# Where the second layer's last 4000 weight columns are loaded, rounded and split

## The reference, cut to what matters

```python
xn = _layernorm(x)
x = x + _L0_attn_ref(xn, ...) + _L0_ffn_ref(xn, ...)   # decay attention; 16 experts, top 2
xn = _layernorm(x)
x = x + _L1_attn_ref(xn, Wqkv, bqkv, Wo, bo) + _L1_ffn_ref(xn, A, B, Wr)
# _L1_attn_ref:
qkv = einsum('bsc,cf->bsf', x, Wqkv) + bqkv
out = softmax(q k^T / sqrt(128)) v;  return out @ Wo + bo
# _L1_ffn_ref:
top_vals, top_idx = top_k(xf @ Wr.T, 16);  gates = softmax(top_vals)
h = einsum('nd,krd->nkr', xf, A)                         # 64 adapters of rank 16
out = einsum('nkr,kdr->nd', h * G[:, :, None], B) * 2.0
```

## Time and profile before

| what | value |
|---|---|
| runs (us) | 2504.53, 2501.66, 2505.94; median 2504.53 |
| profiled execution | 2507.46 us, of it the span 2505.6 us |
| granted TensorE clock, mean | 0.995 |
| busy: PE, PEld, DVE, ACT, POOL | 98%, 85%, 63%, 54%, 63% |
| DMA | 183.87 MB, mean 73 GB/s |
| 2200 to 2220 us: PE busy | 2.16 us of 20 |

### The profile page before, as it was taken

The page is one execution under the profiler, slowest core; times in us unless marked ns, Lnnn a source line. Parts: engine busy times, 40 slices in busy tenths (PEclk is TensorE's granted clock), DMA queues, the critical chain, the costliest instruction groups (busy, mean ns, idle before and its releaser), DMA issues.

```text
span 2505.6 us, 42357 instructions
## 1 busy us (share of the span) xinstructions
PE 2447.8 (98%) x13850; PEld 2120.9 (85%) x13850; DVE 1574.2 (63%) x2449; ACT 1359.2 (54%) x2696; POOL 1582.6 (63%) x1523
## 2 busy tenths in 40 slices
PE   8999999999999999999999999999999999969999
PEld 6888888898989898788888888898888878857787
DVE  6565565757574657876556565757565778865553
ACT  5556555556565555555656555656555557743332
POOL 5666767676676764767776777777686578741210
PEclk9999999999999999999999999999999999989999
DMA  4210211111111113211111111111111178941110
GB/s 161 86 56 30 63 53 39 54 46 54 38 59 42 52 46 101 86 55 56 36 58 54 38 54 46 54 38 59 42 54 44 47 267 293 298 134 42 34 34 34
DMA packets 89196, 183.87 MB, mean 73 GB/s; under 512 B 12626, under 2 KB 38882, under 8 KB 89110
## 3 DMA queue, kind: packets, MB, share of 16 engines
q1 hardware_dynamic: 80566, 165.94, 20.5%
q0 software_dynamic: 8544, 16.82, 2.3%
HBM read 163.81 MB, written 26.79 MB: 76 GB/s over the span
## 4 chain that ended last, share of the span: by engine, by line
PE 86%; DVE 5%; issue 3%; SPq 3%; DMA 1%; ACT 1%; POOL 1%; DVEq 0%; POOLq 0%; ACTq 0%
PE bank L103 27%; PE bank L105 26%; PE bank L104 26%; PE bank L1118 2%; PE bank L1145 2%; SPq L2291 1%; DMA exin<-xn_rows,ecur 0%; DMA y_slots<-ey 0%; DVE acc L2880 0%; PE bank L2720 0%; DVE xl L586 0%; POOL acc L2184 0%; DVE el L2444 0%; SPq L2301 0%; PE bank L2731 0%
## 5 line engine op out<-in xcount | busy, mean ns | idle before, releaser
L2040 POOL TENSOR_TENSOR wl<-w_in,wh 128x512 fp32r<-128x512 f32 x510 | 621.9, 1246 | 304.5 <-ACT wh L1444 301.6
L103 PE MATMUL bank<-xh,wh 128*128 128x512 f32 x1400 | 556.9, 398 | 0.6 <-DVE bank L1751 0.5
L105 PE MATMUL bank<-xh,wl 128*128 128x512 f32 x1400 | 545.7, 390 | 0.0
L104 PE MATMUL bank<-xl_sums,wh 128*128 128x512 f32 x800 | 312.3, 390 | 0.0
L105 PEld LDWEIGHTS bank<-xh,wl 128*128 128x128 f32 x1400 | 262.9, 188 | 56.7
L103 PEld LDWEIGHTS bank<-xh,wh 128*128 128x128 f32 x1400 | 263.5, 188 | 52.8 <-DVE bank L1751 4.2
L2058 POOL TENSOR_TENSOR sqacc<-sqacc,sq 128x512 f32<-128x512 f32 x128 | 173.2, 1353 | 198.9 <-ACT sq L1429 194.4
L1444 ACT CAST wh<-w_in 128x512 fp32r<-128x512 f32 x502 | 262.0, 567 | 32.2 <-POOL w_in L534 32.2
L103 PE MATMUL bank<-wh,xh 128*128 128x256 f32 x912 | 259.0, 284 | 0.2
L104 PE MATMUL bank<-wl,xh 128*128 128x256 f32 x912 | 258.2, 283 | 0.0
L1788 DVE TENSOR_TENSOR acc<-bank,acc 128x512 f32<-128x512 f32 x240 | 162.2, 685 | 118.7 <-PE bank L105 116.6
(11 more groups left out here) (387 smaller groups left out, 6379.6 us busy)
## 6 DMA issues: line engine op xcount, KB each, us to landing
w_in<-in_w_pairs_dram SPq DMA_DIRECT2D x100, 512.0 KB, 3.8
o_in<-in_o_pairs_dram SPq DMA_DIRECT2D x32, 512.0 KB, 3.5
eraw<-in_ex_dram SPq DMA_DIRECT2D x31, 513.0 KB
y_slots<-ey SPq DMA_DIRECT2D x30, 512.0 KB
w_in<-in_w_pairs_dram SPq DMA_DIRECT2D x56, 256.0 KB, 3.0
dcur<-in_decay_dram SPq DMA_DIRECT2D x32, 256.0 KB
eraw<-in_ex_dram SPq DMA_DIRECT2D x31, 256.0 KB
out_dram<-acc SPq DMA_DIRECT2D x16, 256.0 KB, 2.0
```

The lines of the kernel that those rows point to most:

```text
L103: pe.matmul(out, wh, mh, start=start and i == 0, stop=False, skip_group_check=True)
L104: pe.matmul(out, wh, ml, start=False, stop=False, skip_group_check=True)
L105: ins = pe.matmul(out, wl, mh, start=False, stop=stop and i == n - 1, skip_group_check=True)
L2040: pool.tensor_tensor(wl[:, cols], w_in[:, cols], wh[:, cols].bitcast(F32), ALU.subtract).then_inc(w_lo, 1)
```

## The change

SP no longer loads the 4000 columns at tile 27. In the second layer it waits until the last gathered rows of group 0 have landed, then issues the four loads of 1000 columns, ahead of `bo` and `sel`. ACT rounds in eight pieces of 500 columns, three ahead of `score` 0, three ahead of `scores_t` and two ahead of `score` 1 of group 0; ahead of the first it waits for all four loads. POOL subtracts in eight pieces: four ahead of the first four gathers of group 1, four ahead of the other four. These last gathers now stand ahead of POOL's bias additions for group 0. PE waits piece by piece in `outputs(0, i)`.

```diff
-LATE = 4
-LATE_COLS = (L_USED - L_CUT) // LATE
+LATE_COLS = (L_USED - L_CUT) // NR
...
             is_tile, i, _, n = tile(r, b, 0)
-            if isinstance(i, int) and i == NTILES - LATE:
-
-                for k in range(LATE):
-                    c = slice(k * LATE_COLS, (k + 1) * LATE_COLS)
-                    sp.dma_start(w1_late[:, c], l1_w[:, L_CUT + c.start:L_CUT + c.stop]).then_inc(dma_l1[0], 16)
...
+    late_high = {("score", 0, 0): (0, 1, 2), ("scores_t", 0, 0): (3, 4, 5), ("score", 0, 1): (6, 7)}
...
             pe.wait_ge(q["v_hl"], NR * g + i + 1)
-            if g == i == 0:
-                pe.wait_ge(lo_late, PIECES + LATE)
+            if g == 0:
+                pe.wait_ge(lo_late, PIECES + i + 1)
...
     def scalar(a):
-
-        a.wait_ge(dma_late, 16 * (-(-PIECES // 2) + LATE))
-        for c, src in late_cols:
-            a.copy(w1h[:, c], w1_late[:, src]).then_inc(a_late, 1)
         for what, g, i in events:
+            for k in late_high.get((what, g, i), ()):
+                cols, src = late_cols[k]
+                if k == 0:
+                    a.wait_ge(dma_late, 16 * ((PIECES + 1) // 2 + NR // 2))
+                a.copy(w1h[:, cols], w1_late[:, src]).then_inc(a_late, 1)
...
     def vector(v):
-        for k, (cols, src) in enumerate(late_cols):
-            v.wait_ge(a_late, PIECES + k + 1)
-            v.tensor_tensor(w1l[:, cols], w1_late[:, src], w1h[:, cols].bitcast(F32), ALU.subtract).then_inc(lo_late, 1)
...
+        def late_low(*ks):
+            for k in ks:
+                cols, src = late_cols[k]
+                pool.wait_ge(a_late, PIECES + k + 1)
+                pool.tensor_tensor(w1l[:, cols], w1_late[:, src], w1h[:, cols].bitcast(F32),
+                                   ALU.subtract).then_inc(lo_late, 1)
...
+        late_low(0, 1, 2, 3)
+        gather(1, 0)
         pool.wait_ge(dma_sel, 80)
...
         for g in range(NG):
+            if g == 0:
+                late_low(4, 5, 6, 7)
+                gather(1, 1)
...
-            if g + 1 < NG:
+            if 0 < g < NG - 1:
                 gather(g + 1, 0)
                 gather(g + 1, 1)
...
         sp.dma_start(bq[:], b_qkv).then_inc(dma_c, 16)
 
+        sp.wait_ge(dma_y[1][TPG - 1], 16)
+        for k in range(NR // 2):
+            c = slice(2 * k * LATE_COLS, 2 * (k + 1) * LATE_COLS)
+            sp.dma_start(w1_late[:, c], l1_w[:, L_CUT + c.start:L_CUT + c.stop]).then_inc(dma_late, 16)
```

More of the change, by code:

```diff
@@ L133, in two_layers @@
         w1_late = nc.alloc_sbuf_tensor_at("l1_w_late", [P, L_USED - L_CUT], F32, offset=w1_at + 4 * (L_ALL + L_CUT))
-        experts_in = (ex, l1_w, xn_dram, y_slots, ident, expert_of, token_at, table_in, w1h, w1l, w1_late)
-        layer_one_in = (w1h, w1l, w1_late, b_qkv, b_o, sel, ident, acc, slot_of, gate_of, y_slots, out_tiles)
+        experts_in = (ex, l1_w, xn_dram, y_slots, ident, expert_of, token_at, table_in, w1h, w1l)
+        layer_one_in = (w1h, w1l, w1_late, l1_w, b_qkv, b_o, sel, ident, acc, slot_of, gate_of, y_slots, out_tiles)
         with ExitStack() as ctx:
@@ L2220, in routed_experts @@
 def routed_experts(nc, new_sem, at, ps, ex, l1_w, xn_dram, y_slots, ident, expert_of, token_at, table_in, w1h, w1l,
-                   w1_late, blocks_end, blocks_used):
+                   blocks_end, blocks_used):
     end = at
@@ L2512, in routed_experts, with layer_one @@
             "stored": [(dma_y[b], 16 * ((NTILES + 1 - b) // 2 + (b == (NTILES - 1) % 2))) for b in range(2)], "late": (dma_l1[0], a_l1, lo_l1)}
-def layer_one(nc, new_sem, at, ps, w1h, w1l, w1_late, b_qkv, b_o, sel_in, ident, acc, slot_of, gate_of, y_slots, out_tiles,
+def layer_one(nc, new_sem, at, ps, w1h, w1l, w1_late, l1_w, b_qkv, b_o, sel_in, ident, acc, slot_of, gate_of, y_slots, out_tiles,
               stored, late):
@@ L2579, in layer_one @@
     late_cols = [(slice(L_CUT + k * LATE_COLS, L_CUT + (k + 1) * LATE_COLS), slice(k * LATE_COLS, (k + 1) * LATE_COLS))
-                 for k in range(LATE)]
+                 for k in range(NR)]
+    late_high = {("score", 0, 0): (0, 1, 2), ("scores_t", 0, 0): (3, 4, 5), ("score", 0, 1): (6, 7)}
     def rows_of(g, i, t):
```

## The result

The changed kernel takes 2511.88 us (median of 7 runs, 2510.27 to 2513.12), the kernel before in the same series 2503.45 (7 runs, 2501.66 to 2505.94): 1.0035 of it, 95% interval 1.0025 to 1.0045. Forecast were 2507.5 us and a range that ends at 2511. So the change is slower by 8.4 us where 3.0 were reckoned, and outside the range. The profiled execution took 2511.59, its span 2509.8.

The account below looks back on a forecast made before the run. The prediction took the DMA queue to bound the seam up to 2200 and DVE from 2250 to 2270. Its terms -1.7, +1.8 and +2.9 summed to +3.0, giving 2507.5 us, with a range of 2502 to 2511.

Parts of the forecast that it names:

- A: DVE's `top` chain beside POOL's second four subtractions: one wait of 1.2 to two of 2.4, taken as +1.8, ends 0 and 5.0.
- B: Group 0's bias additions, now behind the gathers, delay DVE's `l_hl` (0.4) and two `combine` additions (1.25 each): +2.9, ends 0 and 5.0.
- DVE does not pay: Rival: where DVE and POOL meet, POOL waits, so the gain stays: 2502.8 or 2501.9 us; chance 0.20.
- The seam: Between the two stages: without four loads behind tile 27, ACT's wait for the long store goes; -1.7, bounds 0 and 2.0.
- The first gather: Second layer's first gather, 1.87 us beside DVE's subtraction: counted 0, with 0.9 coming back kept for the range.
- The loads: Four loads behind group 0's last gathered rows: landed at 2230.0, 8.6 us after issue; rival of late landing, chance 0.05.
- ACT's rounding: Eight pieces of 500 columns, 0.5 us each, fit into ACT's idle times in the second layer: cost 0.
- POOL's order: Subtractions, gathers and `sel` copies end at 2248.7, the next gathers start at 2250.03 as before; POOL itself delays nobody.
- The clock: Rival: PE idles above 2 us at DVE's waits make the granted clock fall again, 3.4 on top, 2510.9; chance 0.18.

## Why the prediction was wrong

**The step that failed** is the size of A and B: "A DVE operation with two SBUF operands that meets a POOL operation thus waits for it." I let DVE wait for the operation in hand and take turns with the next. Measured is a wait for the whole row: with three in the row 4.22, with four 4.80 and 5.09, with eight 10.51, with eleven 14.13; and with the row broken by waits 0.74 to 1.8. B was taken as 2.9 and is 4.42. Its place was right, and its size would nearly be right for engines that take turns: with the rows broken the `combine` additions take 3.09 longer (5.82 for 2.73). A was taken as 1.8, and the stretch shows 6.19, of which 4.45 are the wait.

In A the operation was the wrong one as well. By the forecast's own times POOL's second four began at 2243.7, and this stands in before's trace 0.2 us later:

```profile
2243.87 0.62 DVE L2945 TENSOR_SCALAR l_p<-l_p,l_sum 128x256 f32<-128x256 f32 x2
```

The forecast looked for operations with two inputs in SBUF and put the wait at L2919 or L2923, nearly four microseconds later; those with one input it left at "may meet another piece". It is this pair that took 4.80 for 0.35, and when it was through, so was the row.

Did the rows of before mislead me? They did not show the long wait: in that trace no DVE operation waits for more than two of POOL's. They show taking turns also in rows without idle time, GpSimd first, then VectorE:

```profile
63.18 5.11 POOL L2040 TENSOR_TENSOR wl<-w_in,wh 128x512 fp32r<-128x512 f32 x4 [4.98 <-ACT wh L1444]
...
1161.78 4.96 POOL L2040 TENSOR_TENSOR wl<-w_in,wh 128x512 fp32r<-128x512 f32 x4
```

```profile
65.38 0.63 DVE L1728 TENSOR_TENSOR k_lo<-kT,kh 128x256 fp32r<-128x256 f32 x1
66.59 1.10 DVE L1732 TENSOR_TENSOR q_lo<-qT,qh 128x512 fp32r<-128x512 f32 x1 [0.58 <-PE bank L1118]
...
1163.85 2.30 DVE L1768 SCALAR_TENSOR_TENSOR yl<-yf,little,yh 128x512 fp32r<-128x512 f32 x1
```

The first two each got in when the operation in hand had ended, the second and the third of a row of four; ACT had rounded all of the row's pieces before either came. The third waited for the end of the row's third operation and got in ahead of the fourth. In the second layer the small `l_mx` (0.91, in seven traces) and the pair at `l_p` beside the two copies (in three) did not wait for a row's end either. So "the whole row" is what twelve long waits in the second layer show, behind rows of additions and subtractions of 500 or 512 columns; it is no rule for every row, and what decides between the two stays open. No run here tests it.

A row also stood in before's second layer where DVE was seen to get in, first VectorE's timeline, then GpSimd's:

```profile
2273.37 0.69 DVE L2967 TENSOR_TENSOR l_hl<-l_hf,l_hh 128x512 fp32r<-128x512 f32 x1 [0.69 <-ACT l_hh L2831]
```

```profile
2272.16 5.55 POOL L3002 TENSOR_TENSOR acc<-acc,l_bo 128x512 f32<-128x512 f32 x4 [17.39 <-DVE l_stage L2898]
```

`l_hl` starts 0.04 us ahead of the row's second addition and takes 0.69, while POOL's row takes 5.55 instead of 4.99. Here an operation that arrives just between two gets the turn; the three groups' rows repeat this to a few hundredths, and it was half the ground of the rival "DVE does not pay".

**The seam.** -1.7 forecast, -1.73 measured, by the wait that was named. That the two agree so well is in part luck: the three traces with the loads at tile 27 have 8.06, 8.26 and 7.19 us, the seven without 6.30 to 6.33, so the gain is 0.9 to 1.9. The first gather (0, with 0.9 as an end) gives back 0.9: it takes 1.87 in before and 0.96 or 0.97 in the eight traces in which DVE does not subtract beside it. Here I took the wrong end. The stretch to `xt`, -0.91, is not all the gather's, since with the same short gather it lies between 11.90 and 12.75. The section of the Trainium skill cited there (SBUF — State Buffer, Who interferes with whom) had led to 0; the measurement decides.

**The loads** landed earlier than reckoned: issued from 2214.64, they took 3.6 to 5.9 us each, 4.8 in the median, so the last was there some 7.3 us after the first issue, where 8.6 were reckoned, and ACT used them at 2224.75 without a wait. **ACT's rounding** cost nothing, as forecast: 1.64, 1.64 and 1.12 us in its idle times. **POOL's order** came as foreseen: four subtractions, four gathers, the copies of `sel`, four subtractions, four gathers, and then the four additions. The sentence of the Trainium skill that scalings with a single input can take the lock too is borne out: `l_p`, TENSOR_SCALAR, took 4.80 instead of 0.35.

**The clock** fell behind the idle of 4.29, for 3.4 us, and once more behind the one of 5.64, where it cost nothing that shows: the next stretch is 4.63 in kernels with this fall and without it. Its rival was priced at 3.4 and had its place right; it is worth about 1.1 in the first trace of the changed kernel, by the remainder, and 0.8 more in the second, where the clock was down twice as long. The rule "an idle over 2 us" that it used is weak: in the changed kernel's trace one of 2.48 at 2048.92 was followed by no fall.

**The total.** The ends of A and B, 5.0 each, were in the text, and their sum with the gain is +8.3. The range stopped at 2511, the price of the fallen clock, and held no case in which both terms stand at their ends. With one mechanism behind both they are not independent: here DVE waited for the whole row at both places.

## What to carry to other kernels

Reckon with the whole of an unbroken row of GpSimd additions or subtractions on SBUF when you ask what it can do to VectorE: here it held up a TENSOR_TENSOR with both inputs in SBUF, and a TENSOR_SCALAR of 256 columns. It did so in some rows and not in others, so take one operation and the whole row as the two ends, and look in the trace which it was. Put such rows where VectorE is idle for their whole length, and make them wait for its last operation rather than start beside it; where that can't be had, a wait between the operations bounds the damage. When two terms of a sum rest on the same assumption, the range has to hold both at their ends.

## What the runs showed of the hardware that had not been expected

A wait more can make a kernel faster: breaking up the rows took 5.1 us from one stretch. VectorE can stand behind up to eleven GpSimd operations for one of its own, and in other rows takes its turn after one. A VectorE operation that started 0.06 us behind the start of a row of eleven waited 14 us, one that started 0.04 ahead of a row's next operation waited for nothing. The issue of the first gather by POOL took 1.87 and 1.29 us beside VectorE's TENSOR_TENSOR with both inputs in SBUF, and 0.96 to 0.97 without it. The experts' stage took 165 to 172 us in ten traces with the same instructions, up to the `ehf` of tile 27: a difference of one or two microseconds elsewhere can't be read from the spans of single traces.
